# Layer norms of an attention block moved into the next block's softmax part, with the block loops peeled

## The reference

```python
q, k, v = (split_heads(hidden_states @ W + b) for W, b in ((Wq, bq), (Wk, bk), (Wv, bv)))
scores = jnp.einsum('bhqd,bhkd->bhqk', q, k) / scale
...
scores = scores + (c2p + p2c) / scale      # q and k against pos_k, gathered by bucket of q - k
probs = jax.nn.softmax(scores, axis=-1)
ctx = jnp.einsum('bhqk,bhkd->bhqd', probs, v)
out = ctx @ Wo + bo + hidden_states
out = (out - mu) * jax.lax.rsqrt(var + LN_EPS) * ln_scale + ln_bias
...
x = _layernorm(x + _L0_attn_ref(x, ...))   # then the cross attention and the experts, likewise
```

## Time and profile before

| | us |
|---|---|
| median of 3 runs | 3373.96 |
| the runs | 3367.3, 3373.96, 3380.09 |
| the profiled execution | 3373.04 |
| its span, first to last instruction | 3371.3 |
| PE busy in the span | 2793.6 |
| ACT busy | 2484.1 |
| DVE busy | 2369.1 |
| POOL busy | 532.4 |

### The profile page before, as it was taken

How to read it: one execution, slowest core, us unless ns; L and a number is a source line. 1 busy time by engine, 2 the same in 40 slices (tenths; PEclk the granted TensorE clock), 3 DMA queues, 4 the chain that set the end, 5 groups by cost and what they waited for, 6 DMA issues and landing times. The chain is left out here.

```text
span 3371.3 us, 65925 instructions
## 1 busy us (share of the span) xinstructions
PE 2793.6 (83%) x18696; PEld 1614.1 (48%) x18696; DVE 2369.1 (70%) x6960; ACT 2484.1 (74%) x4810; POOL 532.4 (16%) x391
## 2 busy tenths in 40 slices
PE   3888888888788832866659999999999999999994
PEld 1666766666676621752324444444434344444442
DVE  4566566666566656668957777777777777777777
ACT  2677776777677734321549999999999999999993
POOL 2111222113221210110111111111111111111112
PEclk7787777887678855768779999999999999999996
DMA  2000000000000010000010000000000000000001
GB/s 66 12 17 9 9 9 12 16 9 9 9 13 15 9 37 0 0 0 0 0 26 0 0 0 0 0 0 0 0 0 0 0 0 0 0 0 0 0 0 50
DMA packets 43801, 27.89 MB, mean 8 GB/s; under 512 B 17203, under 2 KB 40571, under 8 KB 43771
## 3 DMA queue, kind: packets, MB, share of 16 engines
q1 hardware_dynamic: 43771, 27.53, 3.1%
HBM read 9.94 MB, written 4.19 MB: 4 GB/s over the span
## 5 line engine op out<-in xcount | busy, mean ns | idle before, releaser
L1777 DVE TENSOR_TENSOR c_Hl<-c_HF,c_Hh 128x512 f16<-128x512 f32 x1028 | 686.0, 688 | 299.1 <-ACT c_Hh L1669 283.3
L1665 ACT ACTIVATE c_HF<-c_H,c_b 128x512 f32<-128x512 f32 x1028 | 711.0, 692 | 108.2 <-PE c_H L1582 94.5
L1669 ACT ACTIVATE c_Hh<-c_H,c_b 128x512 f16<-128x512 f32 x1028 | 706.5, 687 | 0.0
L1711 POOL TENSOR_TENSOR c_EX<-c_euler,c_D 128x16 f32<-128x16 f32 x65 | 188.5, 2901 | 1390.4 <-DVE c_D L1747 1390.4
L1580 PE MATMUL c_H<-c_Ch,c_W1h 128*128 128x512 f16 x1028 | 394.7, 384 | 0.0
L1581 PE MATMUL c_H<-c_Cl,c_W1h 128*128 128x512 f16 x1028 | 390.6, 380 | 0.0
L1582 PE MATMUL c_H<-c_Ch,c_W1l 128*128 128x512 f16 x1028 | 390.6, 380 | 0.0
L1592 PE MATMUL c_Y<-c_Hh,c_W2l 128*128 128x512 f16 x1024 | 388.6, 380 | 0.0
L1593 PE MATMUL c_Y<-c_Hl,c_W2h 128*128 128x512 f16 x1024 | 388.6, 379 | 0.0
L1591 PE MATMUL c_Y<-c_Hh,c_W2h 128*128 128x512 f16 x1024 | 388.6, 379 | 0.0
L531 ACT ACTIVATE a_E<-a_T,a_nm 128x128 f32<-128x128 f32 x1024 | 326.1, 396 | 28.2 <-DVE a_nm L614 28.2
(11 more groups left out here) (298 smaller groups left out, 4770.0 us busy)
## 6 DMA issues: line engine op xcount, KB each, us to landing
a_QN<-a_QH SPq DMA_DIRECT2D x136, 32.0 KB, 1.8
a_KN<-a_KH SPq DMA_DIRECT2D x136, 32.0 KB, 1.8
out<-d_O SPq DMA_DIRECT2D x16, 256.0 KB, 2.3
a_QN<-a_QL SPq DMA_DIRECT2D x68, 32.0 KB, 1.8
a_KN<-a_KL SPq DMA_DIRECT2D x68, 32.0 KB, 1.8
CUR<-in_ctx SPq DMA_DIRECT2D x1, 1848.0 KB
c_W<-in_L_ffn_W SPq DMA_DIRECT2D x1, 1024.0 KB
b_VIS<-in_L_xattn_W_f SPq DMA_DIRECT2D x1, 512.0 KB, 4.3
```

Of the source, the lines that this page charges most:

```text
L1665: act.activation(HF[:, k % 4, :], bH[k % 4][:, :], ACT.Gelu_apprx_tanh, bias=b1[:, g % EXPERTS, f:f + 1], scale=1.0 / WSCALE).then_inc(hf_ ...
L1669: act.activation(Hh[:, g % 2, f, :], bH[k % 4][:, :], ACT.Gelu_apprx_tanh, bias=b1[:, g % EXPERTS, f:f + 1], scale=1.0 / WSCALE).then_inc( ...
L1777: dve.tensor_tensor(Hl[:, g % 2, f, :], HF[:, k % 4, :], Hh[:, g % 2, f, :], ALU.subtract)\
```

## The change

- On every engine the loop's body becomes a function `body(i)`. It is called once for block 0, in a loop for blocks 1 to 14, and once for block 15 (on SP: once, and a loop up to block 14).
- `first_norm` and `second_norm` of block i - 1 run in the pass of block i, behind `add_positions` of unit 3 and of unit 5. Those of the last block stand behind everything.
- On POOL the two powers of block i - 1 stand behind the copy of XB and ahead of the residuals of block i.
- The last pass (`last=True`) leaves out the preparation: no transposes, projections, bucket tiles, position chunks, evacuations, halves, values, key spread, or DMAs. The first `out_transpose` of that pass waits for the output sum of the pass before (r_ok) in place of the values' copy (vn_ok), since bank M isn't used for values there.
- X loses its four spare rows, and the memset of them goes.

The waits and counts of the semaphores are otherwise as they were. Nothing of the arithmetic changes.

```diff
@@ gpsimd
-            with pool.Fori(0, NBLK) as i:
-                copy_block(i, 1)
-                residuals(i)
-                spread_keys(i, 1)
-                values_out(i, 1)
+            def powers(i):
                 for n in range(2):
                     pool.wait_ge(var_ok.sem, var_ok.at(i, n + 1))
                     pool.tensor_tensor(rstd[:, :], rstd[:, :], half[:, :], ALU.pow).then_inc(rstd_ok.sem, 1)
+
+            def body(i, first=False, last=False):
+                if not last:
+                    copy_block(i, 1)
+                if not first:
+                    powers(i - 1)
+                residuals(i)
+                if not last:
+                    spread_keys(i, 1)
+                    values_out(i, 1)
+
+            body(0, first=True)
+            with pool.Fori(1, NBLK - 1) as i:
+                body(i)
+            body(NBLK - 1, last=True)
+            powers(NBLK - 1)
@@ tensor
-            def out_transpose(i, b):
+            def out_transpose(i, b, last):
                 pe.wait_ge(on_ok.sem, on_ok.at(i, b + 1))
-                if b == 0:
+                if b == 0 and not last:
                     pe.wait_ge(vn_ok.sem, vn_ok.at(i, 2))
+                if b == 0 and last:
+                    pe.wait_ge(r_ok.sem, r_ok.at(i, 0))
...
-                    if u == 0:
+                    if u == 0 and not last:
                         transposes(i, 1)
...
@@ vector
-            with dve.Fori(0, NBLK) as i:
+
+            def body(i, first=False, last=False):
                 for u in range(UNITS + TAIL):
...
+                    if u == 3 and not first:
+                        first_norm(i - 1)
+                    if u == 5 and not first:
+                        second_norm(i - 1)
...
                     if u == UNITS + TAIL - 2:
                         output_sum(i)
-                first_norm(i)
-                second_norm(i)
+
+            body(0, first=True)
+            with dve.Fori(1, NBLK - 1) as i:
+                body(i)
+            body(NBLK - 1, last=True)
+            first_norm(NBLK - 1)
+            second_norm(NBLK - 1)
```

More of the change, by code:

```diff
@@ L257, in _, with body @@
                     sp.dma_start(dst, src).then_inc(loaded, 16)
+            def body(i):
+                stack_queries(i, 1)
+                stack_keys(i, 1)
             stack_queries(0, 0)
             stack_keys(0, 0)
-            with sp.Fori(0, NBLK) as i:
-                stack_queries(i, 1)
-                stack_keys(i, 1)
+            body(0)
+            with sp.Fori(1, NBLK - 1) as i:
+                body(i)
         @block.gpsimd
@@ L461, in _, with body @@
                 position_chunk(0, 0, c)
-            with pe.Fori(0, NBLK) as i:
+            def body(i, last=False):
                 pe.wait_ge(ga_ok.sem, ga_ok.at(i, ga_ok.per))
@@ L472, in _ @@
                         weighted_values(i, u - 4)
-                    if u == 0:
+                    if u == 0 and not last:
                         transposes(i, 1)
-                    if u == 1:
+                    if u == 1 and not last:
                         project_qk(i, 1)
-                    if u == 2:
+                    if u == 2 and not last:
                         project_v(i, 1)
                     for n in range(2 * (u - 6), 2 * (u - 6) + 2):
-                        if 0 <= n < TILES:
+                        if 0 <= n < TILES and not last:
                             bucket_tile(i, 1, n)
                     if u >= 8 and (u - 8) % UPB == 0:
-                        out_transpose(i, (u - 8) // UPB)
+                        out_transpose(i, (u - 8) // UPB, last)
                     if u >= 9 and (u - 9) % UPB == 0:
                         out_project(i, (u - 9) // UPB)
-                    if u >= UNITS:
+                    if u >= UNITS and not last:
                         for c in (2 * (u - UNITS), 2 * (u - UNITS) + 1):
                             position_chunk(i, 1, c)
+            body(0)
+            with pe.Fori(1, NBLK - 1) as i:
+                body(i)
+            body(NBLK - 1, last=True)
         def spread_rows(banks, c, f):
@@ L551, in _, with body @@
                 evacuate(0, 0, c)
-            with act.Fori(0, NBLK) as i:
+            def body(i, last=False):
                 for u in range(UNITS + TAIL):
-                    if u == 0:
+                    if u == 0 and not last:
                         x_columns(i, 1)
-                    if u == 1:
+                    if u == 1 and not last:
                         high_half(i, 1, 0)
@@ L572, in _ @@
                             evacuate(i, 1, c)
+            body(0)
+            with act.Fori(1, NBLK - 1) as i:
+                body(i)
+            body(NBLK - 1, last=True)
         @block.vector
```

13 lines of the change are left out of this document (6 added, 7 removed).

## The result

| | before | after |
|---|---|---|
| median, us | 3375.03 (6 runs, 3367.3 to 3384.19) | 3397.48 (6 runs, 3387.62 to 3401.2) |
| profiled execution, us | 3373.04 | 3401.2 |
| mean granted clock of TensorE | 0.855 | 0.84 |

The changed kernel takes 1.0063 times as long, 95% interval 1.0042 to 1.0085. It is slower by 0.6%, where 3350 us were forecast.

The account below looks back on a forecast made before the run. At block starts, the norms stand ahead of the next block on three engines, and PE waits for XB's copy. Ordinary blocks 0, long blocks -19, last block -4: -23 us from 3373.04, so 3350 us, range 3320 to 3390.

Parts of the forecast that it names:

- what the start gives: Start of blocks 1 to 15: XB copied ahead of the powers, gain up to unit 8 of 4.55 us a block.
- what the norms cost where they stand: Units 3 to 6: first_norm takes 4.04 us on DVE, unit 6 starts at 16.2 us, PE waits 1.8 us.
- what the clock makes of that wait: Behind unit 6: clock about 0.5 for 7 to 14 us, start's 4.5 us given back by unit 9.
- The first rival: Clock stays high after the wait at unit 6: 60 to 79 us less, about 3305 us; chance 0.10.
- From here the old order of events holds, 0.7 us late at most, and the clock has about the history that it had.: From the second batch's weighted values, at 27.3 us for 26.6 before, the block runs on as before.
- ordinary blocks 0: Sum's term for ordinary blocks: 68.3 us each as before, so no gain or loss.
- the long blocks, -19: Excess of a few long blocks in the attention stage, 19 us, taken as saved, with 0 as the other end.
- the last block: Block 15 to the end of the stage, without preparation, at the low clock: 71 us, 4 less.
- Its other end, 53 at the high pace: Last block if PE runs at 2.26 us a unit: 53 us, 22 less.
- The rival of slower: Low clock runs on from unit 6 to 12, 7.4 us a block; with every second block 3403 us; chance 0.13.

Follow-up runs that it names:

- the two filled kernels: Changed kernel with sixteen transposes of the identity ahead of unit 6's scores, 3339.68 us; changed kernel with 18 at the ends of units 14, 15, 17, 18, 3366.91 us.
- the thin one: Changed kernel with eight products of nine columns ahead of unit 6's scores, where another run had sixteen full transposes: 3404.55 us, 1.0043 of the kernel before.
- the kernel that fills the wait: Changed kernel plus sixteen transposes of the identity into bank M ahead of unit 6's scores: 3339.68 us, 0.9900 of the kernel before.
- the peeled kernel: Changed kernel with norms back at the end of the pass and powers at the end of POOL's pass, loops still peeled: 3351.75 us, 0.9945 of the kernel before.
- the kernel with the filled tail: Changed kernel plus 18 transposes of the identity at the ends of units 14, 15, 17 and 18, wait at unit 6 kept: 3366.91 us, 0.9978.
- that of the pieces: Changed kernel with the norms cut into four pieces, behind the adds of units 6, 8, 10 and 12: 3271.19 us, 0.9677 of the kernel before.
- Another kernel with the same loop: Changed kernel, but the last pass prepares a block that nobody reads, as before: 3403.77 us, 1.0080 of the kernel before.

## Where the prediction held, and where it failed

**Held: what the start gives.** The wait for XB is gone and the transposes come 1.25 us after unit 0, as in block 0. With pieces that make no wait, unit 8 is 18.2 us in: 5.4 us less than the 23.66 read from the earlier trace rows, where 4.55 were taken.

**Held: what the norms cost where they stand.** first_norm 4.04 us, unit 6 at 15.5 us (16.2 forecast), PE's wait 1.78 (1.8).

**Held: what the clock makes of that wait.** 0.50 for 6.8 us, forecast 7 to 14, so just at the short end. Unit 8 24.3 us in, forecast 25.2; unit 9 28.3, forecast within 0.7 of 28.9. The first rival, that the clock stays high, was wrong here, and right about the mechanism: where it was made to stay high, the block lost 3.4 us against 68.3 (forecast 2.7).

**Failed: "From here the old order of events holds, 0.7 us late at most, and the clock has about the history that it had."** The order of events did hold, up to unit 15 at 46.9 to 48.6 us (47.8 before). The clock's history did not. I had followed it from unit 6 to unit 9 and then taken the rest of the block from block 8, where the clock was at 1.00 from 692.98 to 699.05. The changed block has it at 0.50 from 490.40 on. The events being in the same places didn't carry the clock with them, and a low clock in the tail costs 4 to 5 us, as the two filled kernels and the thin one show. The term "ordinary blocks 0" is +3.3 us a block, 47 us over fourteen blocks (1003.3 for 956). The way from the wait at unit 6 to the low tail is shown by the kernel that fills the wait, in thirteen blocks of fourteen, and it isn't the only way: block 0 of the change has no norms in it and no wait at unit 6, and its tail took 24.8 us too (20.8 before).

**Failed with it: the long blocks, -19.** There is no block of 75.7 us any more, as said. But the working for that looked only at the middle of the block. In place of many blocks of 68.3 and a few of 70 to 76, all fourteen are long, between 71.3 and 72.3. The price of a low tail could have been read ahead. In the long block of the earlier trace rows, from 221.57 on, unit 15 starts 50.6 us in, and its tail takes 25.2 us where an ordinary one takes 20.6: 4.6 of the 7.4 us lie in the tail, whose first 10.1 us have a clock of 0.69. The prediction put the whole 7.4 on a low stretch that runs on to unit 12.

**Held, in part by luck: the last block,** 71.2 for 71, at a clock of 0.57. The 71 hold 10.3 us for the norms, read to 1204.7, where the last write of X ends at 1203.65; the norms took 8.6 (1218.8 to 1227.4). So the other terms were too small by about 2 us, and the gain is 3.2 us and not 4. Its other end, 53 at the high pace, is near what the peeled kernel has (54.4).

**The rival of slower** had the right sign and nearly the time (3403 for 3397), but named another place, so that its time came out near is luck. Its stretch from unit 6 to 12 ended after 6.8 us in the block shown (in the kernel with the filled tail it did run on, for 24 us); the tail took the time instead. Its chance of 0.13 was too small, because it was priced for one place only, while a shifted clock can cost anywhere in the block.

**Sum.** By the profiled execution 3350 was forecast and 3401.2 came, 51 more: 47 in blocks 1 to 14, 0.8 in the last one and 4.5 in the stages behind, less 0.3 ahead of block 1 and what the terms were rounded by. Why the stages behind take 2172.1 us where they took 2167.65 isn't settled; with the same code they took 2172.4 in the peeled kernel, 2170.7 in that of the pieces and 2166.4 in that with the norms behind units 6 and 8, so it isn't the place of the norms. Nor is it settled what decides at which instruction of a block the clock falls: the runs show that it can be moved by what PE does there, not how to foretell it from the rows of another order.

## What to carry to other kernels

Work moved off the path at one place must not make another engine wait in one long piece. With the last block's gain in all of them, the kernels take 3351.75 us with the norms at their old place, 3397.48 with 4 us of them in one piece behind unit 3, 3342.92 with the same piece behind unit 6, and 3271.19 in four pieces of 1.1 to 1.6 us from unit 6 on. So some of the gain is the place and more of it the cutting. When a change shifts where TensorE waits or works, follow the granted clock to the end of the loop body, not only behind the edit, and look at the stretches with thin matmuls too. A few matmuls that nobody reads can pay: fourteen transposes a block took another 31 us away (3271 to 3240).

## What the runs showed of the hardware that was not expected

- PE busy by the profile for the whole of a stretch (10.10 of 10.10 us) can be at 0.50 of its clock for the whole of it.
- 1.94 us of transposes with 128 columns and 1.93 us of products with nine were followed by clocks of 1.00 and 0.58, and blocks of 64.9 and 71.6 us.
- With a wait of 1.78 us at one place of a block of 70 us the low stretches of all the rest are elsewhere, in a pattern that from block 6 on repeats every three blocks (71.3, 72.2 and 71.6 us; every four in the kernel with the filled tail). Another kernel with the same loop has blocks of 68.0 us among them.
- Two waits of 1.67 us at the same weighted values were followed by clocks of 0.57 (before, at 667.92) and of 1.00 (with the pieces, at 621.78), each over 4.0 us.
- 18 added transposes a block can make the kernel 31 us faster (3397.48 to 3366.91), and 8 thin products 88 us slower (3351.75 to 3440.17).
